# The late expert tiles of a gated transformer block, from 256 rows of one expert to two pieces of 128

## The chip, the cores and the metric

The kernel runs on one NeuronCore of one Trainium2 chip. The core has TensorE (PE in the profile; its weight loads stand apart as PEld), VectorE (DVE), ScalarE (ACT), GpSimd (POOL), SyncE (SP, which here only issues transfers) and 16 DMA engines. The metric is the device time of one execution in microseconds. It is the median of the runs.

## The reference, cut to what matters

x and ctx are 128 sequences of 64 tokens with 128 values each, 8192 tokens in all.

```python
x = x + tanh(g_xattn) * attention(layernorm(x), ctx, ctx)    # 16 heads of 8
z = layernorm(x)                                              # per token
logits = z @ gate_kernel                                      # 8 experts
top_w, top_i = top_k(logits, 2); w = softmax(top_w)
for each token, for each of its two experts n:
    h = silu(z @ w0_kernel[n]) * (z @ w1_kernel[n])           # 128 -> 256
    y += w[n] * (h @ wo_kernel[n])                            # 256 -> 128
x = x + tanh(g_ffn) * y
```

Everything is float32. Each token goes to two of eight experts, so the experts have 16384 rows to work through. How many fall to which expert is known only at run time.

## The kernel before, in words

**Two stages.** The attention stage goes over 64 tiles of 128 tokens in a software pipeline. For each token it also finds the two experts and scatters two copies of the normalised row, with the token's number and weight behind it (130 values, 520 bytes), into `lists` in DRAM: there each expert has a list of its own, filled from the front (POOL, indirect DMA, line 1114). Fills of padding rows (line 294) stand behind each list; their token number is out of bounds, so that their result is dropped.

The expert stage goes over `NET` = 71 tiles of `ET` = 256 rows. A tile belongs to one expert. Since every list but for luck ends within a tile, there are 64 + 7 tiles: 2 x 8192 / 256 and up to seven more. The stages overlap: after 48 token tiles (`EARLY`) a count shows how many full tiles each expert has, and a first table lists `NFULL` = 41 of them, for which all rows are there. A second table, made by DVE while the first expert tiles run (`second_table`, lines 851 to 898), lists the other 30 from the final counts. A table has two rows: the expert of each tile and its first row in `lists`.

**One expert tile t.** Every engine runs the same steps s, each with its own offset:

- SP (`take`, lines 365 to 374) reads the first row from the table into a register, waits until the scatter of tile t - 8 has landed and the outputs of tile t - 6 are made, and issues the load of 256 rows into `zin` (8 buffers).
- PE in step s turns the rows of tile s + 2 (`rows_turned`, L546), multiplies tile s + 1 with the first layer's weights (`first_products`, L556, two matrices of 256 columns into two PSUM banks) and tile s with the second layer's (`second_layer`, L572). For the latter it reads the expert's number into a register (`expert`, recorded at L298) and addresses `wo` with it. A float32 matmul is two passes in the profile, each with its own weight load.
- ACT in step s reads the expert's number of tile s + 2 and copies that expert's two first matrices into `wcur` (L720), does the silu of tile s + 1 (L726) and scales the outputs of tile s by the token's weight (L733).
- DVE in step s copies the turned rows of tile s + 2 (L1015) and multiplies silu and second product of tile s + 1 (`hm`, L1022).
- POOL scatters the 2 x 128 result rows of tile s to `results`, by token number (L1170). In the first 20 steps it also scatters the last eight half tiles of the lists (L1114).

Steps below `steady` = 18 are written out, steps 18 to 49 are a loop of four turns of eight tiles, and the rest is written out again; the order of the work on each engine is the order of these calls.

**The end.** Once all tiles below `NEARLY` = 55 have landed, every result of the first 48 token tiles is in `results`: SP fetches them in 12 chunks of four token tiles (L379), one after each `take`, DVE adds them up in steps from `COMBINE_AT` = 60 on (L1028, L1030), and ACT issues the stores (L739). The last four chunks are fetched when all 71 tiles have landed.

Of the kernel before, what the change touches and what calls it, by code (L numbers as in the profile page):

```python
# [13 lines left out]
P = 128  # L14
# [7 lines left out]
SPARE = E  # L22
# [3 lines left out]
NET = 2 * NT * P // ET + E - 1  # L26
NFULL = 2 * EARLY * P // ET - (E - 1)
NEARLY = 2 * EARLY * P // ET + (E - 1)
# [59 lines left out]
EXPERTS = Pipeline(NET, behind=1, ahead=2, unroll=8, steady=18, turns=4)  # L88
# [34 lines left out]
def flamingo_block(nc, A, out):  # L123
    with ExitStack() as ctx:
# [111 lines left out]
        left = sb("left", [P, E])  # L236
# [10 lines left out]
        tile_no = sb("tile_no", [P, NET])  # L247
# [10 lines left out]
        wcur = sb("wcur", [P, 2, 2, HID])  # L258
# [46 lines left out]
        EARLY_READY, LATE_READY = 11, 20  # L305
# [4 lines left out]
        with nc.Block() as block:  # L310
            @block.sync
            def _(sp):
# [52 lines left out]
                def take(t):  # L365
                    row = sp.value_load(table[0:1, 1, t.val:t.val + 1] if isinstance(t.val, int) else table[0:1, 1, bass.ds(t.val, 1)],
                                        min_val=0, max_val=ZROWS - ET)
# [6 lines left out]
                    sp.dma_start(zin[:, t.buf(8), :, :], lists[bass.ds(row, ET), :].rearrange("(p h) c -> p h c", h=2)).then_inc(z_in[t.buf(8)], 16)  # L374
# [54 lines left out]
            def _(pe):  # L429
# [119 lines left out]
                def first_products(s):  # L549
                    if t := EXPERTS.at(s, 1):  # L550
# [668 lines left out]
```

## Time and profile before

| | us |
|---|---|
| median of 3 runs (lowest, highest) | 565.22 (564.27, 565.32) |
| the profiled execution | 563.8 |
| its span in the profile | 562.0 |
| PE busy | 536.1 |
| ACT busy | 411.7 |
| DVE busy | 401.4 |
| POOL busy | 375.9 |

The span runs from the first to the last instruction of the profiled execution; the 1.8 us around it are in the execution's own time. The busy time of an engine is the time in which at least one of its instructions ran. Register loads, waits and the issuing of transfers are not counted in it. The views used below are the page; the timeline, which gives instructions in order of time with the idle time before them and what ended it; the view of one source line, which also has the sequencer's own instructions (marked q); the waits; and busy times by window.

### The profile page before, as it was taken

The page shows a single profiled execution, that of the slowest core. Times are in us where ns is not written, and L with a number is a line of the kernel's source. Part 1 is how long each engine was busy: PE and PEld are TensorE (multiplying, and loading weights), DVE is VectorE, ACT ScalarE, POOL GpSimd, SP SyncE. Part 2 cuts the span into 40 slices and gives each one's busy share as a digit, 9 for nine tenths or more (in the row PEclk, how much of TensorE's full clock was granted, in tenths as well). Part 3 has the DMA queues.
Part 4 walks back from the last instruction along what each step waited for, and adds up shares of the span by engine and source line. Part 5 has one row for each costly group of instructions (what it writes and reads, how often), then busy time and mean ns, then how long its engine had stood idle before and what let it go on. Part 6 is the DMA issues. An engine that isn't in the chain of part 4 may idle for free.

```text
span 562.0 us, 20142 instructions
## 1 busy us (share of the span) xinstructions
PE 536.1 (95%) x5964; PEld 456.0 (81%) x5965; DVE 401.4 (71%) x1356; ACT 411.7 (73%) x1083; POOL 375.9 (67%) x520
## 2 busy tenths in 40 slices
PE   8999999999999999999999999999899999999960
PEld 6888787888888887888788778998889999999950
DVE  5888988998898998898999875473333333335773
ACT  4788888888888888888999896666566656665630
POOL 3237676767767767677776765777777776667770
PEclk9999999999999999999999999999999999999985
DMA  3652121121222212212212222334333333338997
GB/s 89 207 150 77 55 86 59 52 80 56 66 66 66 75 56 72 69 52 82 60 58 80 78 59 67 100 98 145 112 101 101 106 99 95 94 91 229 314 302 224
DMA packets 70249, 58.00 MB, mean 103 GB/s; under 512 B 8966, under 2 KB 66062, under 8 KB 70192
## 3 DMA queue, kind: packets, MB, share of 16 engines
q1 hardware_dynamic: 52672, 35.98, 22.7%
q0 software_dynamic: 8640, 16.93, 8.9%
q10 hardware_dynamic: 8880, 4.39, 2.6%
q8 instruction: 27, 0.44, 0.4%
q14 instruction: 30, 0.25, 0.1%
HBM read 29.84 MB, written 24.15 MB: 96 GB/s over the span
## 4 chain that ended last, share of the span: by engine, by line
PE 72%; POOL 10%; issue 9%; DMA 4%; DVE 2%; POOLq 1%; ACT 1%; SPq 0%; ACTq 0%; DVEq 0%
PE psO L526 12%; PE psH L466 12%; POOL results L1170 9%; PE psH L556 9%; PE psH L452 7%; PE psH L458 7%; PE psK L504 5%; PE psO L484 3%; PE psX L471 3%; PE psO L498 3%; PE psG L572 2%; PE psO L572 2%; DMA results<-ys,zin 2%; PE psX L508 1%; PE psK L479 1%
## 5 line engine op out<-in xcount | busy, mean ns | idle before, releaser
L1170 POOL DMA_INDIRECT results<-ys,zin x142 | 139.6, 983 | 50.6 <-issue 47.2
L1114 POOL DMA_INDIRECT lists<-zp,dest x128 | 128.1, 1001 | 61.4 <-DVE dest L922 28.9
L556 PE MATMUL psH<-zT,wcur 128*128 128x256 f32 x568 | 134.6, 380 | 0.0
L556 PEld LDWEIGHTS psH<-zT,wcur 128*128 128x128 f32 x568 | 102.4, 190 | 11.2 <-issue 0.2
L1022 DVE TENSOR_TENSOR hm<-psH,hs 128x512 f32<-128x512 f32 x71 | 49.1, 692 | 85.5 <-PE psH L556 52.3
L658 ACT ACTIVATE ex<-psH,rs 128x512 f32<-128x512 f32 x128 | 81.2, 684 | 38.6 <-PE psH L458 38.6
L907 DVE TENSOR_REDUCE mx<-psH 128x8 fp32r<-128x512 f32 x128 | 82.5, 686 | 4.4 <-PE psH L452 0.3
L526 PEld LDWEIGHTS psO<-v,pT 128*64 128x64 f32 x2048 | 65.0, 138 | 25.1 <-issue 23.1
L466 PE MATMUL psH<-ident,ex 128*128 128x128 f32 x512 | 76.4, 282 | 0.1
L526 PE MATMUL psO<-v,pT 128*64 128x64 f32 x2048 | 73.7, 225 | 0.6 <-ACT pT L662 0.6
L1153 POOL TENSOR_TENSOR kvr<-ropA,ropB 128x256 f32<-128x256 f32 x64 | 46.4, 726 | 40.1 <-DVE ropB L984 23.8
L662 ACT COPY pT<-psH 128x512 f32<-128x512 f32 x128 | 72.9, 600 | 0.2
L702 ACT COPY v<-kvr 64x64 f32<-64x64 f32 x256 | 63.3, 247 | 2.3
L466 PEld LDWEIGHTS psH<-ident,ex 128*128 128x128 f32 x512 | 54.0, 140 | 13.2 <-ACT ex L658 10.2
L458 PE MATMUL psH<-mx,minus 128*128 128x256 f32 x256 | 59.8, 320 | 0.0
L720 ACT COPY wcur<-w 128x512 f32 x71 | 43.8, 617 | 11.5 <-issue 7.9
L733 ACT ACTIVATE ys<-psO,zin 128x128 f32<-128x128 f32 x72 | 22.5, 363 | 32.9 <-PE psO L572 32.9
L932 DVE TENSOR_TENSOR kmask<-psK,hmask 128x512 f32<-128x512 f32 x64 | 44.0, 687 | 3.1 <-PE psK L479 2.5
L733 ACT ACTIVATE ys<-psG,zin 128x128 f32<-128x128 f32 x70 | 21.9, 363 | 32.9 <-PE psG L572 31.9
L452 PE MATMUL psH<-kmask,qT 32*64 32x256 f32 x1024 | 44.6, 400 | 0.0
L726 ACT ACTIVATE hs<-psH 128x512 f32<-128x512 f32 x71 | 42.0, 591 | 2.8 <-PE psH L556 2.8
L458 PEld LDWEIGHTS psH<-mx,minus 128*128 128x128 f32 x256 | 38.5, 190 | 3.6 <-DVE mx L907 0.2
(157 smaller groups left out, 991.8 us busy)
## 6 DMA issues: line engine op xcount, KB each, us to landing
zin<-lists SPq DMA_DIRECT2D x71, 130.0 KB, 2.1
yy<-results SPq DMA_DIRECT2D x16, 512.0 KB, 5.8
xres<-x1r SPq DMA_DIRECT2D x32, 128.0 KB, 2.2
out_dram<-xres ACTq DMA_DIRECT2D x16, 256.0 KB, 3.9
xring<-in_x_dram SPq DMA_DIRECT2D x31, 128.0 KB, 2.2
cring<-in_ctx_dram SPq DMA_DIRECT2D x31, 128.0 KB, 2.3
results<-ys,zin POOLq DMA_INDIRECT x142, 2.5
lists<-pad SPq DMA_DIRECT2D x16, 130.0 KB, 3.4
```

Source lines behind the costliest of these rows:

```text
L452: last = pe.matmul(psH[h][c, g % 2, 0:256], qT[r, t.buf(2), c], kmask[r, t.buf(2), :, c], start=True, stop=False, skip_group_check=True)
L458: last = pe.matmul(psH[h][:, g % 2, 0:256], minus[:, :], mx[:, 4 * g:4 * g + 4].unsqueeze(2).broadcast_to([P, 4, S]), start=False, stop=Tr ...
L466: last = pe.transpose(psH[h][:, n // 2, o:o + P], ex[:, t.buf(2), h, n * P:(n + 1) * P], ident[:, :])
L526: last = pe.matmul(psO[b * S:(b + 1) * S, n * VW:n * VW + VPAD], pT[:, t.buf(2), n // 4, o:o + S], v9[:, t.buf(4), b, n * VW:n * VW + VPAD ...
L556: last = pe.matmul(bank[t.buf(2)][:, k * ET:(k + 1) * ET], wcur[:, t.buf(2), a, k * P:(k + 1) * P], zT[:, t.buf(2), :], start=True, stop=True)
L658: nc.scalar.activation(ex[:, t.buf(2), h, :].rearrange("p (g c) -> p g c", g=2), psH[h][:, :, 0:256], ACT.Exp, scale=rs[:, t.buf(4) // 2, ...
L662: nc.scalar.copy(pT[:, t.buf(2), h, :].rearrange("p (g c) -> p g c", g=2), psH[h][:, :, 256:512]).then_inc(p_sb[h], 1)
L702: last = nc.scalar.copy(dst, src)
L907: nc.vector.tensor_reduce(mx[:, 8 * h:8 * h + 8].rearrange("p (g n) -> p g n", g=2), psH[h][:, :, 0:256].rearrange("p g (n k) -> p g n k", ...
L1022: nc.vector.tensor_tensor(hm[:, t.buf(2), :, :].rearrange("p k t -> p (k t)"), psB[t.buf(2)][:, :], hs[:, t.buf(2), :], ALU.mult).then_inc ...
L1114: nc.gpsimd.indirect_dma_start(lists, bass.IndirectOffsetOnAxis(ap=dest[:, t.buf(4), j:j + 1], axis=0), zp[:, t.buf(4), j, :], None).then_ ...
L1170: nc.gpsimd.indirect_dma_start(results, bass.IndirectOffsetOnAxis(ap=zin[:, t.buf(8), h, D:D + 1].bitcast(U32), axis=0), ys[:, t.buf(8), h ...
```

## The change

Tiles 0 to 40 stay. From tile 41 on (the 42nd) a tile of 256 rows is two pieces of 128 rows, each with an expert and a first row of its own in the table. Lists are thus rounded up to 128 rows behind the first table's tiles, and 68 tiles hold them: (128 + 7 + 1) // 2. The second table has 54 entries, one for each piece, in place of 30. A late tile is loaded with two transfers; ACT copies two experts' matrices; the first layer's matmuls are made for 128 columns at a time, each with the weights of its piece; the second layer uses each piece's expert. `NEARLY` goes from 55 to 52. The loop has two turns instead of four, so that no late tile lies in it. PE and ACT wait for the second table at the steps 41 and 39 instead of 17 and 15.

```diff
-SPARE = E
+SPARE = E // 2
 ZROWS = E * CAP + SPARE * ET
 ROW = D + 2
 EARLY = 3 * NT // 4
-NET = 2 * NT * P // ET + E - 1
 NFULL = 2 * EARLY * P // ET - (E - 1)
-NEARLY = 2 * EARLY * P // ET + (E - 1)
+NET = (2 * NT + E - 1 + 1) // 2
+NEARLY = (2 * EARLY + E - 1 + 1) // 2
+PIECES = 2 * (NET - NFULL)
+NTAB = NFULL + PIECES
...
-EXPERTS = Pipeline(NET, behind=1, ahead=2, unroll=8, steady=18, turns=4)
+EXPERTS = Pipeline(NET, behind=1, ahead=2, unroll=8, steady=18, turns=2)
...
-        past = sb("past", [P, NET - NFULL, SEG])
-        hop = sb("hop", [P, 2, NET - NFULL, SEG])
-        tfl = sb("tfl", [P, 2, NET])
-        first_row = sb("first_row", [P, NET])
-        table = sb("table", [P, 2, NET], U32)
+        past = sb("past", [P, PIECES, SEG])
+        hop = sb("hop", [P, 2, PIECES, SEG])
...
-        wcur = sb("wcur", [P, 2, 2, HID])
+        wcur = sb("wcur", [P, 2, 2, 2, HID])
...
-        def expert(eng, t):
-
-            return eng.value_load(table[0:1, 0, t.val:t.val + 1] if isinstance(t.val, int) else table[0:1, 0, bass.ds(t.val, 1)],
-                                  min_val=0, max_val=E - 1)
+        def late(t):
+
+            return t.turn is None and t.k >= NFULL
+
+        def entry(t, h):
+            if late(t):
+                k = NFULL + 2 * (t.k - NFULL) + h
+                return slice(k, k + 1)
+            return slice(t.val, t.val + 1) if isinstance(t.val, int) else bass.ds(t.val, 1)
+
+        def rows_there(eng, t):
+
+            if late(t):
+                slot = range(t.buf(8), t.k + 1, 8)
+                eng.wait_ge(z_in[t.buf(8)], sum(32 if n >= NFULL else 16 for n in slot))
+            else:
+                wait_slot(eng, z_in, t, 16)
+
+        def expert(eng, t, h=0):
+
+            return eng.value_load(table[0:1, 0, entry(t, h)], min_val=0, max_val=E - 1)
...
-                    row = sp.value_load(table[0:1, 1, t.val:t.val + 1] if isinstance(t.val, int) else table[0:1, 1, bass.ds(t.val, 1)],
-                                        min_val=0, max_val=ZROWS - ET)
+                    rows = [sp.value_load(table[0:1, 1, entry(t, h)], min_val=0, max_val=ZROWS - (P if late(t) else ET))
+                            for h in range(2 if late(t) else 1)]
                     wait_slot(sp, y_out, t, 32, back=8)
                     carry(sp)
                     if t.turn is not None or t.k >= 8:
                         wait_for(sp, y_sb, t, back=6)
                     carry(sp)
                     carry(sp)
-                    sp.dma_start(zin[:, t.buf(8), :, :], lists[bass.ds(row, ET), :].rearrange("(p h) c -> p h c", h=2)).then_inc(z_in[t.buf(8)], 16)
+                    if late(t):
+                        for h in range(2):
+                            sp.dma_start(zin[:, t.buf(8), h, :], lists[bass.ds(rows[h], P), :]).then_inc(z_in[t.buf(8)], 16)
+                    else:
+                        sp.dma_start(zin[:, t.buf(8), :, :], lists[bass.ds(rows[0], ET), :].rearrange("(p h) c -> p h c", h=2)).then_inc(z_in[t.buf(8)], 16)
...
-                        wait_slot(pe, z_in, t, 16)
+                        rows_there(pe, t)
...
-                                last = pe.matmul(bank[t.buf(2)][:, k * ET:(k + 1) * ET],
-                                                 wcur[:, t.buf(2), a, k * P:(k + 1) * P],
-                                                 zT[:, t.buf(2), :], start=True, stop=True)
+                                for h, c in enumerate((slice(0, P), slice(P, ET)) if late(t) else (slice(0, ET),)):
+                                    last = pe.matmul(bank[t.buf(2)][:, k * ET + c.start:k * ET + c.stop],
+                                                     wcur[:, t.buf(2), h, a, k * P:(k + 1) * P],
+                                                     zT[:, t.buf(2), c], start=True, stop=True)
...
-                        e = expert(pe, t)
+                        e = [expert(pe, t, h) for h in range(2)] if late(t) else [expert(pe, t)] * 2
...
-                                                 wo[:, bass.ds(e, 1), k, :].squeeze(1), start=(k == 0), stop=(k == 1))
+                                                 wo[:, bass.ds(e[h], 1), k, :].squeeze(1), start=(k == 0), stop=(k == 1))
...
-                    if static(s, EXPERTS.steady - 1):
+                    if static(s, NFULL):
...
-                        e = expert(act, t)
+                        e = [expert(act, t, h) for h in range(2 if late(t) else 1)]
                         wait_for(act, b_ps, t, back=2)
-                        nc.scalar.copy(wcur[:, t.buf(2), :, :], w01[:, bass.ds(e, 1), :, :].squeeze(1)).then_inc(w_done, 1)
+                        for h, n in enumerate(e):
+                            last = nc.scalar.copy(wcur[:, t.buf(2), h, :, :], w01[:, bass.ds(n, 1), :, :].squeeze(1))
+                        last.then_inc(w_done, 1)
...
+                        nc.vector.tensor_copy(ecnt[:, :], psG[:, 0:E])
...
-                        nc.vector.tensor_scalar(ntu[:, 1, :], ntu[:, 0, :], ET.bit_length() - 1, None, ALU.logical_shift_right).then_inc(late_table, 1)
                         dve.wait_ge(late_table, 4)
+                        nc.vector.tensor_scalar(ntu[:, 1, :], ntu[:, 0, :], P.bit_length() - 1, None, ALU.logical_shift_right).then_inc(late_table, 1)
+                        nc.vector.tensor_scalar(ecu[:, 1, :], ecu[:, 0, :], P.bit_length() - 1, None, ALU.logical_shift_right).then_inc(late_table, 1)
+                        dve.wait_ge(late_table, 6)
                         nc.vector.tensor_copy(ntf[:, :], ntu[:, 1, :]).then_inc(late_table, 1)
-                        dve.wait_ge(late_table, 5)
-                        nc.vector.tensor_tensor(left[:, :], ntf[:, :], seg_len[:, 0:E], ALU.subtract).then_inc(late_table, 1)
+                        nc.vector.tensor_copy(ecf[:, :], ecu[:, 1, :]).then_inc(late_table, 1)
+                        nc.vector.tensor_scalar(seg_len[:, 0:E], seg_len[:, 0:E], 2.0, None, ALU.mult).then_inc(late_table, 1)
                     if n == 2:
-                        dve.wait_ge(late_table, 6)
-                        nc.vector.tensor_scalar(seg_len[:, E:2 * E], left[:, :], 1.0, None, ALU.min).then_inc(late_table, 1)
-                        dve.wait_ge(late_table, 7)
-                        nc.vector.tensor_tensor(seg_len[:, 2 * E:SEG], left[:, :], seg_len[:, E:2 * E], ALU.subtract).then_inc(late_table, 1)
-                        nc.vector.scalar_tensor_tensor(out=seg_row[:, E:2 * E], in0=seg_len[:, 0:E], scalar=float(ET), in1=seg_row[:, 0:E],
+                        dve.wait_ge(late_table, 9)
+                        nc.vector.tensor_tensor(seg_len[:, E:2 * E], ecf[:, :], seg_len[:, 0:E], ALU.subtract).then_inc(late_table, 1)
+                        nc.vector.tensor_tensor(seg_len[:, 2 * E:SEG], ntf[:, :], ecf[:, :], ALU.subtract).then_inc(late_table, 1)
...
-                        nc.vector.tensor_tensor(past[:, :, :], seg_end[:, :].unsqueeze(1).broadcast_to([P, late, SEG]),
-                                                tile_no[:, NFULL:NET].unsqueeze(2).broadcast_to([P, late, SEG]), ALU.is_le).then_inc(late_table, 1)
+                        dve.wait_ge(late_table, 16)
+                        nc.vector.tensor_tensor(past[:, :, :], seg_end[:, :].unsqueeze(1).broadcast_to([P, PIECES, SEG]),
+                                                tile_no[:, NFULL:NTAB].unsqueeze(2).broadcast_to([P, PIECES, SEG]), ALU.is_le).then_inc(late_table, 1)
```

The remaining edits name the new buffers, make the two iotas of the tables in two parts each, and renumber the semaphore counts of `second_table` (`LATE_READY` 23 instead of 20).

## Rows read from the trace of the kernel before

**Rows 1.** The profile page: busy time of PE, and the clock granted in 40 slices

```profile
PE 536.1 (95%) x5964; PEld 456.0 (81%) x5965; DVE 401.4 (71%) x1356; ACT 411.7 (73%) x1083; POOL 375.9 (67%) x520
...
PEclk9999999999999999999999999999999999999985
```

**Rows 2.** Timeline of one late tile, all engines: start, duration in us, [idle before]

```profile
492.30 1.05 PE L572 MATMUL psO<-wo,hm 128*128 x8
492.50 0.69 DVE L1022 TENSOR_TENSOR hm<-psH,hs 128x512 f32<-128x512 f32 x1 [1.30 <-PE psH L556]
...
493.19 0.38 PE L546 MATMUL psK<-ident,zin 128*128 128x128 f32 x2
...
493.39 0.62 ACT L733 ACTIVATE ys<-psO,zin 128x128 f32<-128x128 f32 x2 [1.01 <-PE psO L572]
493.40 1.89 PE L556 MATMUL psH<-zT,wcur 128*128 128x256 f32 x8
...
494.10 0.62 ACT L720 COPY wcur<-w 128x512 f32 x1
...
494.62 0.59 ACT L726 ACTIVATE hs<-psH 128x512 f32<-128x512 f32 x1
494.83 0.97 POOL L1170 DMA_INDIRECT results<-ys,zin  x1 [0.59 <-issue]
...
495.13 1.05 PE L572 MATMUL psG<-wo,hm 128*128 x8
```

**Rows 3.** Timeline of PE alone from 403 to 420 us

```profile
404.37 0.44 PE L546 MATMUL psX<-ident,zin 128*128 128x128 f32 x2 [1.45 <-DMA zin<-lists]
...
416.26 0.44 PE L546 MATMUL psX<-ident,zin 128*128 128x128 f32 x2 [0.32 <-DMA zin<-lists]
...
418.50 1.05 PE L572 MATMUL psO<-wo,hm 128*128 x8
```

**Rows 4.** Timeline of POOL from 360 to 366 us

```profile
361.10 0.97 POOL L1170 DMA_INDIRECT results<-ys,zin  x1 [0.30 <-issue]
362.38 0.97 POOL L1170 DMA_INDIRECT results<-ys,zin  x1 [0.30 <-issue]
363.66 0.96 POOL L1114 DMA_INDIRECT lists<-zp,dest  x1 [0.30 <-issue]
```

**Rows 5.** Line 298 on PE's sequencer, 492.2 to 493.1: min/median/max ns, first and last start

```profile
L298 PEldq TENSOR_LOAD <-table x1: 297/297/297, 492.3 to 492.3; - x1
...
L298 PEldq SEQ_ASSERT  x1: 18/18/18, 492.9 to 492.9; - x1
```

**Rows 6.** Line 572 on PE's sequencer, 492 to 495 us

```profile
L572 PEldq FUSED_REGOPS  x2: 46/46/46, 493.2 to 493.4; - x2
```

**Rows 7.** Register loads of line 298 on PE, 430 to 520, then 520 to 542

```profile
L298 PEldq TENSOR_LOAD <-table x32: 297/302/419, 430.4 to 517.9; - x32
...
L298 PEldq TENSOR_LOAD <-table x8: 302/618/1217, 520.7 to 539.3; - x8
```

**Rows 8.** Timeline of ACT near the end: a store's issue

```profile
535.97 0.39 ACTq L739 DMA_DIRECT2D out_dram<-xres  x1
```

**Rows 9.** Timeline of DVE from 370 to 378 us

```profile
377.02 0.89 DVE L894 TENSOR_REDUCE tfl<-hop 128x30 f32<-128x720 f32 x1
```

**Rows 10.** Waits of SP, 430 to 500: us in total, times, longest us

```profile
SPq L120 <- DMA results<-ys,zin: 22.3, 26, 2.0
```

**Rows 11.** Timeline of SP from 506 to 532 us

```profile
508.83 0.44 SPq L379 DMA_DIRECT2D yy<-results  x1
...
530.38 1.77 SPq L379 DMA_DIRECT2D yy<-results  x2
```

**Rows 12.** Busy time of each engine in a window, then granted clock, DMA share, GB/s

```profile
core 0: us, PE busy (x) PEld busy (x) DVE busy (x) ACT busy (x) POOL busy (x), PEclk, DMA share, GB/s
530.00:540.00 10.00, 10.00 (x64) 9.23 (x63) 8.40 (x15) 6.18 (x15) 6.79 (x7) 1.00 1.04 334
```

**Rows 13.** Waits of SP from 500 us to the end

```profile
SPq L120 <- DMA results<-ys,zin: 11.6, 8, 2.2
```

More of the change, by code:

```diff
@@ L235, in flamingo_block @@
         ntf = sb("ntf", [P, E])
-        left = sb("left", [P, E])
+        ecnt = sb("ecnt", [P, E])
+        ecu = sb("ecu", [P, 2, E], U32)
+        ecf = sb("ecf", [P, E])
         seg_len = sb("seg_len", [P, SEG])
@@ L246, in flamingo_block @@
         padrow = sb("padrow", [P, E], U32)
-        tile_no = sb("tile_no", [P, NET])
+        tile_no = sb("tile_no", [P, NTAB])
         early_past = sb("early_past", [P, NFULL, E])
         early_hop = sb("early_hop", [P, NFULL, E])
-        past = sb("past", [P, NET - NFULL, SEG])
-        hop = sb("hop", [P, 2, NET - NFULL, SEG])
-        tfl = sb("tfl", [P, 2, NET])
-        first_row = sb("first_row", [P, NET])
-        table = sb("table", [P, 2, NET], U32)
+        past = sb("past", [P, PIECES, SEG])
+        hop = sb("hop", [P, 2, PIECES, SEG])
+        tfl = sb("tfl", [P, 2, NTAB])
+        first_row = sb("first_row", [P, NTAB])
+        table = sb("table", [P, 2, NTAB], U32)
         warm = sb("warm", [P, 1])
@@ L849, in second_table @@
                 def second_table(n):
-                    late = NET - NFULL
                     if n == 0:
@@ L888, in second_table @@
+                        nc.vector.tensor_tensor(hop[:, 0, :, :], past[:, :, :], expert_step[:, :].unsqueeze(1).broadcast_to([P, PIECES, SEG]),
                                                 ALU.mult).then_inc(late_table, 1)
[L889 removed]
+                        nc.vector.tensor_tensor(hop[:, 1, :, :], past[:, :, :], jump[:, :].unsqueeze(1).broadcast_to([P, PIECES, SEG]),
                                                 ALU.mult).then_inc(late_table, 1)
@@ L891, in second_table @@
                     if n == 6:
-                        dve.wait_ge(late_table, 16)
-                        nc.vector.tensor_reduce(tfl[:, 0, NFULL:NET], hop[:, 0, :, :], AX_X, ALU.add).then_inc(late_table, 1)
-                        nc.vector.tensor_reduce(tfl[:, 1, NFULL:NET], hop[:, 1, :, :], AX_X, ALU.add).then_inc(late_table, 1)
+                        dve.wait_ge(late_table, 19)
+                        nc.vector.tensor_reduce(tfl[:, 0, NFULL:NTAB], hop[:, 0, :, :], AX_X, ALU.add).then_inc(late_table, 1)
@@ L895, in second_table @@
+                        nc.vector.tensor_reduce(tfl[:, 1, NFULL:NTAB], hop[:, 1, :, :], AX_X, ALU.add).then_inc(late_table, 1)
                     if n == 7:
-                        dve.wait_ge(late_table, 18)
-                        nc.vector.tensor_scalar(table[:, 0, NFULL:NET], tfl[:, 0, NFULL:NET], float(E - 1), None, ALU.min).then_inc(late_table, 1)
-                        nc.vector.tensor_tensor(table[:, 1, NFULL:NET], tfl[:, 1, NFULL:NET], first_row[:, NFULL:NET], ALU.add).then_inc(late_table, 1)
+                        dve.wait_ge(late_table, 21)
@@ L900, in rows @@
+                        nc.vector.tensor_scalar(table[:, 0, NFULL:NTAB], tfl[:, 0, NFULL:NTAB], float(E - 1), None, ALU.min).then_inc(late_table, 1)
+                        nc.vector.tensor_tensor(table[:, 1, NFULL:NTAB], tfl[:, 1, NFULL:NTAB], first_row[:, NFULL:NTAB], ALU.add).then_inc(late_table, 1)
                 def rows(t):
@@ L1088, in _ @@
                 pool.wait_ge(pad_ready, 1)
-                nc.gpsimd.iota(tile_no[:, :], pattern=[[1, NET]], base=0, channel_multiplier=0,
+                nc.gpsimd.iota(tile_no[:, 0:NFULL], pattern=[[1, NFULL]], base=0, channel_multiplier=0,
+                               allow_small_or_imprecise_dtypes=True)
+                nc.gpsimd.iota(tile_no[:, NFULL:NTAB], pattern=[[1, PIECES]], base=2 * NFULL, channel_multiplier=0,
                                allow_small_or_imprecise_dtypes=True).then_inc(e_const, 1)
-                nc.gpsimd.iota(first_row[:, :], pattern=[[ET, NET]], base=0, channel_multiplier=0,
+                nc.gpsimd.iota(first_row[:, 0:NFULL], pattern=[[ET, NFULL]], base=0, channel_multiplier=0,
+                               allow_small_or_imprecise_dtypes=True)
+                nc.gpsimd.iota(first_row[:, NFULL:NTAB], pattern=[[P, PIECES]], base=2 * NFULL * P, channel_multiplier=0,
                                allow_small_or_imprecise_dtypes=True).then_inc(e_const, 1)
```

24 lines of the change are left out of this document (11 added, 13 removed).

## The prediction, made before the changed kernel was run

> **What bounds the kernel now.** The page comes first: TensorE (PE) is busy 95% of the span, and the granted clock stands at nine tenths or more of 2.4 GHz up to the last two of 40 slices [rows 1]. So PE looks like the bound, but a busy share is an average, and the change touches only the last stage. The timeline of one expert tile there comes next [rows 2]: second layer (L572), two transposes (L546), eight matmul passes of the first layer (L556), next second layer, without a gap. From the second layer at 418.50 [rows 3] to that at 492.30 [rows 2] there are 26 tiles in 73.80 us, 2.84 us each. In each, PE spends 1.73 us on L556 (493.40 to 495.13, 8 x 0.216), 0.89 on L572 (492.30 to 493.19, 8 x 0.111) and 0.21 on L546. ScalarE (ACT) is free for 1 us before each result, GpSimd (POOL) for 0.59.
>
> Is PE the bound of the whole stage? No: at 404.37 and 416.26 it waited 1.45 and 0.32 us for rows [rows 3]. The reader should see POOL behind this: its scatters follow each other every 1.28 us, and eight scatters of the last lists (L1114) are mixed in [rows 4]. Two scatters of results are 2.56 us a tile, so POOL gains back 0.28 us a tile once the extra ones are done, and by the tile of rows 2 it idles. Up to about the 26th tile POOL sets the pace, afterwards PE. The change replaces tiles from the 42nd on: all of them lie in PE's part.
>
> **What is removed.** NET goes from 71 to 68: three tiles of 2.84 us, and NEARLY and COMBINE_AT move down by three too (55 to 52, 60 to 57), so that the fetches and sums keep their place relative to the last tile, and what lies behind it stays. Gain: 3 x 2.84 = 8.5 us.
>
> **PE's added work.** In 27 late tiles the first layer is split by columns: 16 passes of 128 columns, each with its weights, in place of 8 of 256. No first-layer pass of 128 columns is in the trace, but L572 is the same shape (128x128 weights, 128 columns, float32) at 0.111: 16 x 0.111 = 1.78 against 1.73, +0.05 a tile. The bounds are 16 x 0.107 (L546's, no more than before) and 16 x 0.112: 0 to +0.06. I take 0.05: 27 x 0.05 = 1.4 us. Late period: 2.89.
>
> **PE's second register load.** A late tile reads two expert numbers. The first costs PE's sequencer 0.30 us for the load at 492.3 and, with the range check at 492.9, about 0.67 in all, 0.37 beside the load [rows 5]. Then come the address computations of L572, at 493.2 and 493.4 [rows 6]. This load belongs to the second layer that runs at 495.13. It starts when PE begins the second layer before, with 8 + 2 + 8 = 18 matmuls still queued: so the sequencer runs some 16 to 18 matmuls ahead, no more. Today these are 2.83 us of work over about 1.1 us of sequencer time. After the change the 16 short L556 passes fill that room alone: the loads can start only when the second transpose's weights are taken, 0.9 us after L572's start; they take 2 x (0.37 + load), and some 0.25 follows until the first matmul is handed over. With today's lead of weights (0.1) the loop of the sequencer is 0.9 + 0.74 + 2 x load + 0.35 = about 2.0 + 2 x load. At 0.30 that is 2.6, hidden under 2.89 with 0.3 to spare. But from 520 us on the same load takes 0.62 in the median of eight, up to 1.22 [rows 7]: 2.0 + 1.24 = 3.25, or 0.36 over 2.89. Bounds for the seven or eight tiles there: 0 (only the first of the pair is slow and the next catches up) to 8 x 0.36 = 2.9; I take the middle, 1.4.
>
> The Trainium skill, DMA: Bandwidth & Descriptors, Latency and other measured facts, gives a register load a floor of about 600 ns. The trace disagrees for most of the stage, 0.30, and comes to such a figure only at the end. By that rule the loop would be 3.2 in all 27 tiles and the gain gone (rival 2). The skill's Advanced Engine Details and Errata, Engine Queue Depths, gives TensorE a queue of 64; counted as weight loads and matmuls, the trace shows about half. By that depth the second load would be hidden even at 1.2 us (rival 1).
>
> **ACT.** It copies weights twice. One copy occupies it 0.52 (494.10 to the silu at 494.62). The second load adds about 0.6 (493.39 to 494.10 is 0.71 today, load and checks). So silu starts 0.71 + 0.6 + 1.04 = 2.35 after the outputs and leaves ACT at about 2.85: just under 2.89. Silu comes 1.1 us later than today; the product (hm, 0.69) behind it would end about 3.7 after the outputs' start, and its second layer starts at 4.7 (today hm ends 2.6 after, its consumer starts 4.6 after). Hidden, with 1 us left. In the last 11 steps ACT also issues the stores, 0.39 each [rows 8], ahead of its loads. It can work through that, since a late ACT finds its result waiting and loads while the silu still runs: 0. If that cover is gone: 0.4 x 11 = 4.3 us.
>
> **VectorE (DVE).** The second table gets 54 x 24 = 1296 elements for 720. At 0.90 us each [rows 9] the five operations grow by about 0.6 each, 3 us together, in three steps of 2.84, two of them ahead of a tile's transposed input. One tile is late by up to 1.3 us around 378 us. That lies in POOL's part: PE then waits less for rows at 404.37 [rows 3]. 0 us; 1.3 if POOL were not the pace there. The small added operations (one copy in the attention stage, some on eight elements) I put at 0.1 together, the two extra iotas and four fewer fills at 0.
>
> **SP and DMA.** A late tile is two transfers of 128 x 520 B for one of 128 x 1040 B: the same bytes, one more issue of 0.33 and a second load, about 1.1 us more of SP a tile. From 430 to 500 SP spends 22.3 us in 26 waits for scatters to land [rows 10], most of them behind the load, and it works up to eight tiles ahead: hidden. In the last steps it also fetches results; the fetches come every 3.1 us (seven steps from 508.83 to 530.38) [rows 11], slower than PE's tiles, with the DMA engines full [rows 12]. In its eight waits for scatters there SP spends 11.6 us, 1.4 each [rows 13], which would hold the 1.1; but the second issue comes behind the wait. Bounds 0 and 8 x 0.5 = 4 us; as the waits are the longer I take 0.3.
>
> **Sum.** -8.5 + 1.4 + 1.4 + 0.3 + 0.1 = -5.3 us. Against the profiled execution, 563.8 (span 562.0), that is 558.5; against the median of the runs shown, 565.22, it is **559.9 us**. I give the second.
>
> **Rivals.** (1) *Only the matmuls cost.* The slow loads and SP stay hidden: -8.5 + 1.4 + 0.1 = -7.0, 558.2. For it: the 0.3 us to spare in PE's loop, and SP's waits. Against it: loads of 0.62. The Trainium skill's queue of 64 would lead here too.
> (2) *PE waits for its register loads, or ACT for its own, in every late tile.* Place: PE's sequencer between first and second layer, tiles 41 to 67. Price: with loads of 0.62 throughout, 3.25 - 2.84 = 0.41 x 27 = 11.1, against 8.5: +2.6, 567.9, slower. It decides from a period of 2.84 + 8.5/27 = 3.16, that is from loads of 0.58. Against it: 32 loads of 0.30 in the median from 430 to 520 [rows 7]. It is what the Trainium skill's floor of a register load (the page named above) would do here.
> (3) *The same, partly*: period 3.0 to 3.1, because handing over costs more than I count or ACT's 2.85 is really 3.0. 27 x 0.2 = 5.4 instead of 1.4: -8.5 + 5.4 + 1.8 = about -1.5, 563.7. From -2 up to no change.
> (4) *The end is DMA's.* With the engines full from 510 on, three tiles less do not bring the fetches forward; then the end stays at its place, and only slack goes: about 565. Against it: the first fetch waits for the scatters of the first NEARLY tiles, which come three tiles earlier, and the last four fetches start only behind the last scatter, in the old kernel as in the new.
>
> **Chances.** Forecast (-4 to -6.5): 0.45. Rival 1 (-6.5 to -8): 0.25. Loss between (-1.1 to -4, rival 3): 0.13. Rival 4 or rival 3 at its end, within 1.1 us: 0.08. Rival 2: 0.09. A measurement of this kernel tells about 0.2%, 1.1 us, from no change: faster 0.83, same 0.08, slower 0.09. Range: low, near rival 1 without a price for the matmuls (556.8), 557.0; high, rival 3, 563.7; outside are rival 2, rival 4 and a little below: 2 in 10.
>
> **What would show it.** L572 to L572 of late tiles 2.89 before the fetches and 2.9 to 3.3 after; 16 passes of L556 in 1.78; two loads behind each other on PE with the first at the second transpose; ACT's wait for PE shrunk from 1.0 to nearly 0; silu 2.35 behind the outputs; SP's waits shorter. Wrong would be: a gap of PE before L572 in tiles 41 to 58, loads of 0.6 there, or the last scatter not earlier by 5 us.

## The result, and the profile after

Twenty runs of each kernel were compared: 561.86 us after (559.71 to 564.4), 565.18 before (563.4 to 567.21). The ratio is 0.9946, 95% interval 0.9936 to 0.9957. By it the change takes 3.05 us off (2.4 to 3.6), where 5.3 were predicted; the medians are 3.3 apart. The profiled execution took 560.92 us, its span is 558.8.

The page, busy times and granted clock (after; it answers to [rows 1]):

```profile
PE 531.9 (95%) x6126; PEld 456.5 (82%) x6127; DVE 399.4 (71%) x1354; ACT 419.4 (75%) x1098; POOL 370.3 (66%) x516
...
PEclk9999999999999999999999999999999999999995
```

PE is busy 4.2 us less, ACT 7.7 us more. The timeline of PE in the first late tiles (after; start, duration in us):

```profile
459.77 1.06 PE L598 MATMUL psO<-wo,hm 128*128 x8
460.66 0.38 PE L571 MATMUL psK<-ident,zin 128*128 128x128 f32 x2
460.88 1.95 PE L582 MATMUL psH<-zT,wcur 128*128 128x128 f32 x16
462.67 1.06 PE L598 MATMUL psG<-wo,hm 128*128 x8
```

L571, L582 and L598 are the old L546, L556 and L572. From second layer to second layer is 2.90 us. The sixteen first-layer passes take 462.67 - 460.88 = 1.79, against 1.73 for the eight of [rows 2]. This goes on without a gap for nineteen tiles. In the last eight it does not (PE's timeline, after):

```profile
515.95 2.02 PE L582 MATMUL psH<-zT,wcur 128*128 128x128 f32 x16
518.13 1.15 PE L598 MATMUL psO<-wo,hm 128*128 x8 [0.17 <-issue]
...
519.55 2.05 PE L582 MATMUL psH<-zT,wcur 128*128 128x128 f32 x16
521.55 1.15 PE L598 MATMUL psG<-wo,hm 128*128 x8
...
532.28 2.05 PE L582 MATMUL psH<-zT,wcur 128*128 128x128 f32 x16 [0.33 <-ACT wcur L747]
534.53 1.15 PE L598 MATMUL psG<-wo,hm 128*128 x8 [0.20 <-issue]
...
537.31 1.06 PE L598 MATMUL psO<-wo,hm 128*128 x8
539.25 1.15 PE L598 MATMUL psG<-wo,hm 128*128 x8 [0.89 <-ACT ys L761]
```

Follow one late pair. The second layer at 518.13 should have come at 517.74, 2.90 behind that at 514.84; it is 0.39 late. What held it is not in PE's own timeline but in its sequencer. The instructions there, from the trace (start, us, ns, engine):

```
515.987   383 Tensor  TENSOR_LOAD  L320 <-table
516.720   763 Tensor  TENSOR_LOAD  L320 <-table
516.361   302 Scalar  TENSOR_LOAD  L320 <-table
516.920  1074 Scalar  TENSOR_LOAD  L320 <-table
517.297   961 Sync    TENSOR_LOAD  L387 <-table
...
519.622   303 Tensor  TENSOR_LOAD  L320 <-table
```

PE's second register load ends at 517.48, and behind it come its checks and the addresses of L598. ACT's second load ends at 517.99, its weight copies start at 518.36, and the next L582 waits for them (timeline of all engines, after):

```profile
518.12 0.97 PEld L598 LDWEIGHTS psO<-wo,hm 128*128 128x128 f32 x8 [0.35 <-issue]
...
518.36 1.14 ACT L747 COPY wcur<-w 128x512 f32 x2 [1.49 <-PE psH L582]
...
519.54 0.19 PEld L582 LDWEIGHTS psH<-zT,wcur 128*128 128x128 f32 x1 [0.28 <-ACT wcur L747]
```

So in this pair each engine's second load has a part. L598 is 0.39 late behind PE's own loads, the first of which had itself begun 0.24 late. Then L582 follows 1.42 behind L598 in place of 1.11, 0.31 late by `wcur`. PE's next loads (519.62, the second of 0.72) begin only behind that L582, and the next L598 loses another 0.21: 0.39 and 0.52 over 2.90 in two tiles. The waits of the last stretch (after, 511 to 541; us in total, times, longest) show the same two causes. `issue` before a weight load is PE's sequencer that hands over late, here behind its register loads:

```profile
PEld psG L598 <- issue: 1.5, 2, 1.1
PEld psH L582 <- ACT wcur L747: 1.1, 3, 0.6
PE psG L598 <- ACT ys L761: 0.9, 1, 0.9
PEld psO L598 <- issue: 0.4, 1, 0.4
```

The 1.1 of `issue` and the 0.9 of `ys` are one gap, that ahead of the last tile. It is PE's own, since the outputs that this tile needs, those of the tile two before, were ready at 536.35: no L582 covers the last tile's two loads (0.80 and 0.30, from 537.26 on). The sequencer of PE over the two stretches (line 320, which [rows 7] has as line 298; min/median/max ns, first and last start):

```profile
L320 PEldq TENSOR_LOAD <-table x42: 295/300/482, 439.9 to 510.0; - x42
...
L320 PEldq TENSOR_LOAD <-table x16: 297/304/947, 516.0 to 538.4; - x16
```

The median stays at 0.30 to the end: of sixteen loads, five are slow (0.51 to 0.95), four of them the second of their pair. The windows (after; the one of 530 to 540 answers to [rows 12]) show when this begins, with the DMA engines full:

```profile
core 0: us, PE busy (x) PEld busy (x) DVE busy (x) ACT busy (x) POOL busy (x), PEclk, DMA share, GB/s
440.00:500.00 60.00, 60.00 (x496) 58.77 (x495) 22.05 (x42) 43.25 (x99) 42.62 (x45) 1.00 0.35 98
...
510.00:520.00 10.00, 9.79 (x85) 9.33 (x84) 6.98 (x12) 6.78 (x17) 6.75 (x7) 1.00 0.97 283
520.00:530.00 10.00, 9.99 (x87) 9.62 (x86) 7.73 (x14) 6.95 (x17) 5.83 (x6) 1.00 1.03 316
530.00:540.00 10.00, 8.58 (x72) 7.97 (x71) 8.18 (x14) 5.63 (x13) 6.15 (x6) 1.00 0.98 304
```

PE is busy for sixty of sixty us, and from 530 on for 8.58 of ten. SP's waits from 430 to 500, where [rows 10] had 22.3 us in one row, and the last scatter of POOL:

```profile
SPq L122 <- DMA results<-ys,zin: 9.5, 8, 1.4
SPq L122 <- ACT ys L761: 7.2, 13, 0.8
```

```profile
543.90 0.97 POOL L1203 DMA_INDIRECT results<-ys,zin  x1 [0.30 <-issue]
```

Before, that scatter was issued at 547.10: it is 3.2 us earlier. From its end to the end of the span both kernels need 13.9 us.

**The account of the two profiled executions**, by the first second-layer matmul of each tile:

| | before | after | difference |
|---|---|---|---|
| first tile starts | 341.19 | 342.31 | +1.12 |
| first to 41st tile | 117.05 | 117.46 | +0.41 |
| 41st to the ninth last | 62.44 (22 x 2.84) | 55.07 (19 x 2.90) | -7.37 |
| ninth last to last | 20.68 | 24.42 | +3.74 |
| last tile to last scatter | 5.74 | 4.64 | -1.10 |
| from there to the end | 14.9 | 14.9 | 0 |

They sum to -3.2, the difference of the spans. Each column is one execution.

### The profile page after: what moved, and what is told of

The parts are those of the page before. It is cut to its first block, busy times and chain, and to the rows that moved or that the text cites. A ratio compares the mean times of both kernels' runs of the same rounds, so it can differ in the third digit from the quotient of the medians.

```text
span 558.8 us, 20707 instructions
## 1 busy us (share of the span) xinstructions
PE 531.9 (95%) x6126; PEld 456.5 (82%) x6127; DVE 399.4 (71%) x1354; ACT 419.4 (75%) x1098; POOL 370.3 (66%) x516
## 4 chain that ended last, share of the span: by engine, by line
PE 86%; ACT 3%; issue 3%; DMA 3%; ACTq 2%; DVE 2%; POOL 1%; POOLq 0%; SPq 0%; DVEq 0%
PE psH L582 17%; PE psO L551 12%; PE psH L491 12%; PE psH L477 7%; PE psH L483 7%; PE psK L529 5%; PE psG L598 4%; PE psO L598 4%; PE psO L509 3%; PE psX L496 3%; PE psO L523 3%; ACTq L320 1%; PE psX L533 1%; PE psK L504 1%; PE psX L534 1%
## 5 line engine op out<-in xcount | busy, mean ns | idle before, releaser
L1203 POOL DMA_INDIRECT results<-ys,zin x136 | 133.8, 984 | 52.2 <-issue 42.1
L582 PE MATMUL psH<-zT,wcur 128*128 128x128 f32 (+1 forms) x760 | 131.0, 321 | 1.1 <-issue 0.7
L582 PEld LDWEIGHTS psH<-zT,wcur 128*128 128x128 f32 x760 | 109.5, 191 | 8.9 <-issue 1.1
L1051 DVE TENSOR_TENSOR hm<-psH,hs 128x512 f32<-128x512 f32 x68 | 47.0, 691 | 91.7 <-PE psH L582 46.6
L747 ACT COPY wcur<-w 128x512 f32 x95 | 56.0, 616 | 23.9 <-issue 19.3
L754 ACT ACTIVATE hs<-psH 128x512 f32<-128x512 f32 x68 | 40.2, 591 | 3.4 <-PE psH L582 3.3
L529 PE MATMUL psK<-wT,xcT 128*128 128x256 f32 x128 | 38.7, 384 | 1.1 <-DVE kmask L961 1.1
L678 ACT ACTIVATE zp<-x1r,nmr,rs 128x256 f32<-128x256 f32 x64 | 38.5, 602 | 1.5
```

Of the source, the lines that this page charges most:

```text
L529: pe.matmul(psK[:, 0:2 * D], xcT[:, t.buf(8), P:2 * P], wT[:, 1:3, :], start=True, stop=True).then_inc(kv_ps, 1)
L582: last = pe.matmul(bank[t.buf(2)][:, k * ET + c.start:k * ET + c.stop], wcur[:, t.buf(2), h, a, k * P:(k + 1) * P], zT[:, t.buf(2), c], st ...
L1203: nc.gpsimd.indirect_dma_start(results, bass.IndirectOffsetOnAxis(ap=zin[:, t.buf(8), h, D:D + 1].bitcast(U32), axis=0), ys[:, t.buf(8), h ...
```

## The experiments

Twelve runs were made of six kernels, in four groups, each on one chip. The kernel before took 664.6, 684.4, 564.9 and 663.1 us there: three groups met chips on which it takes 1.17 to 1.21 times as long, and there PE doesn't set the pace of the tiles. So the third group, on a chip like the one of the result, carries the verdicts; its four kernels are those of the first. The changed kernel itself was not in it: it is compared with the others by its ratio of 0.9946 from the first comparison. Each ratio is to the kernel before on the same chip, with its 95% interval.

### Three tiles fewer and nothing else

```diff
-NET = 2 * NT * P // ET + E - 1
+NET = 2 * NT * P // ET + E - 1 - 3
-NEARLY = 2 * EARLY * P // ET + (E - 1)
+NEARLY = 2 * EARLY * P // ET + (E - 1) - 3
```

> The kernel before with 68 tiles in place of 71 and nothing else changed (the last three tiles' rows are left out of the computation). Theory (the three tiles are worth 2.84 us each, and what follows the last tile stays where it was relative to it): 8.5 us less than before, a ratio of 0.985. Rival 4 (the transfers set the end): 0 to 2 us less.

Measured: 654.46 us against 664.56, ratio 0.9832 [0.9807, 0.9856].

> The kernel before with 68 tiles in place of 71 and nothing else; three tiles' work (and so three tiles' rows) is left out. Where TensorE sets the pace, three tiles at a period of 2.84 us make 8.5 us less: 556.7 against 565.2 (ratio 0.985). If the end belonged to the transfers, it would be within 2 us of the kernel before.

Measured: 556.67 us, ratio 0.985 [0.9824, 0.9876], that is -8.5 us (the span is 8.2 less). The first term of the sum holds. Rival 4, by which the end is the transfers', falls: the last scatter is issued at 537.91, 9.2 earlier, and 1.0 of that is lost again behind it.

### The split matmuls alone

```diff
-EXPERTS = Pipeline(NET, behind=1, ahead=2, unroll=8, steady=18, turns=4)
+EXPERTS = Pipeline(NET, behind=1, ahead=2, unroll=8, steady=18, turns=2)
...
+                                late = t.turn is None and t.k >= NFULL
+                                for c in (slice(0, P), slice(P, ET)) if late else (slice(0, ET),):
-                                last = pe.matmul(bank[t.buf(2)][:, k * ET:(k + 1) * ET],
+                                    last = pe.matmul(bank[t.buf(2)][:, k * ET + c.start:k * ET + c.stop],
                                                  wcur[:, t.buf(2), a, k * P:(k + 1) * P],
-                                                 zT[:, t.buf(2), :], start=True, stop=True)
+                                                     zT[:, t.buf(2), c], start=True, stop=True)
```

The late steps are written out (turns=2), and the tables are those of the kernel before; the first sentence of the second text below says otherwise, and is wrong in that.

> The kernel before with its 71 tiles of one expert; only the first layer's matmuls from tile 41 on are made for 128 columns at a time, and the loop has two turns, so that these tiles are written out. Theory: 0.06 us for each of 30 late tiles, 1.7 us more than before, period 2.90, no gaps of TensorE. Rival (handing over twice as many matmuls costs something at the end, where register loads are slow): 3 to 5 us more.

Measured: 667.69 us against 664.56, ratio 1.0041 [1.0024, 1.0058].

> The kernel before, its 71 tiles kept, from the 42nd on with the products of a tile made in pieces of 128 columns and the tables built as in the changed kernel, but with one expert number for a tile, so without any further load of a number. If the split matmuls are all that the late tiles cost, the rise is 30 tiles x 0.06 = 1.8 us (567.0, ratio 1.003), and the rest of the late tiles' price, which the trace of the changed kernel puts at 3.7 us in the last eight, comes from the second loads. If the split alone brings that too, +4 to +5 us (569.5).

Measured: 566.3 us, ratio 1.0023 [1.0004, 1.0041], +1.3 us. Every interval between second layers from the 41st tile on is 2.90, the last eight included, up to the last two of 2.68 and 1.03. The last eight sum to 21.1 us against 20.7 before. PE's timeline at the end (split alone):

```profile
536.76 1.06 PE L574 MATMUL psG<-wo,hm 128*128 x8
539.66 1.06 PE L574 MATMUL psO<-wo,hm 128*128 x8
542.34 1.06 PE L574 MATMUL psG<-wo,hm 128*128 x8
```

So the split costs what its 0.06 a tile says, and the gaps of the last eight tiles are not its doing.

### One expert number for both pieces

```diff
-                        e = [expert(pe, t, h) for h in range(2)] if late(t) else [expert(pe, t)] * 2
+                        e = [expert(pe, t)] * 2
...
-                        e = [expert(act, t, h) for h in range(2 if late(t) else 1)]
+                        e = [expert(act, t)] * (2 if late(t) else 1)
```

> The changed kernel, in which TensorE and ScalarE read one expert number for a late tile and use it for both pieces (the second piece is computed with the first one's expert). Theory (the 3.7 us lost in the last eight tiles come from the second register load on the two sequencers): about 3 us less than the changed kernel, a ratio to before of 0.989 to 0.990, last eight tiles at 2.9. Rival (ScalarE's second copy, the second transfer and the full DMA engines do it): no more than 1 us less than the changed kernel, 0.994.

Measured: 661.8 us against 664.56, ratio 0.9955 [0.9923, 0.9987].

> As the run of the same kernel above (one expert number for both pieces on TensorE and ScalarE), now beside the changed kernel: by the theory 3 us less than the changed kernel (0.5%), by the rival less than 1 us.

Measured: 682.49 us against 684.42, ratio 0.9899 [0.9851, 0.9947].

> The changed kernel with one expert number read for both pieces of a tile by TensorE and ScalarE, so that the second piece is multiplied with the first piece's weights. If the second loads cost the 3.7 us that the last eight tiles took more than before, less 0.5 for the split, this gains 2 to 3.2 us on the changed kernel (559.2, ratio to the kernel before 0.989 to 0.990). If the loads cost nothing and the end is the split's or the transfers', it is the changed kernel again (0.9946).

Measured: 559.87 us, ratio 0.9904 [0.9878, 0.993], so 2.4 us less than the changed kernel (0.9946 [0.9936, 0.9957]; the two intervals just don't overlap, and the 2.4 could be 0.8 to 4). PE's timeline at the end (one number):

```profile
529.19 1.06 PE L598 MATMUL psO<-wo,hm 128*128 x8
...
532.09 1.06 PE L598 MATMUL psG<-wo,hm 128*128 x8
...
534.77 1.06 PE L598 MATMUL psO<-wo,hm 128*128 x8
535.98 1.15 PE L598 MATMUL psG<-wo,hm 128*128 x8 [0.15 <-DVE hm L1051]
```

The 2.90 stand to the end. The last eight intervals sum to 21.28 us, against 24.42 in the changed kernel: 3.14 us are the second reads' of PE and ACT together (load, check and addresses). The span shrinks by 2.1 only, since POOL is then the later at the end: its last scatter stands 5.94 behind the last tile and not 4.64. SP's second load, both transfers of a tile and ACT's second copy are still in this kernel, so they cost PE nothing here. The windows of the two kernels have nearly the same DMA share (1.04 and 1.03 from 520 to 530), so it isn't that the DMA engines are less full (one number):

```profile
520.00:530.00 10.00, 10.00 (x92) 10.00 (x91) 7.91 (x14) 8.11 (x18) 7.96 (x7) 1.00 1.04 316
```

### The loads moved apart

The whole of the changed kernel; on PE the first number is read ahead of the first products, on ACT the second is read behind the first copy.

```diff
-                def second_layer(s):
+                def second_layer(s, e0=None):
-                        e = [expert(pe, t, h) for h in range(2)] if late(t) else [expert(pe, t)] * 2
+                        e = [e0, expert(pe, t, 1)] if late(t) else [expert(pe, t)] * 2
...
+                    t0 = EXPERTS.at(s, 0)
+                    e0 = expert(pe, t0, 0) if t0 and late(t0) else None
...
-                        e = [expert(act, t, h) for h in range(2 if late(t) else 1)]
-                        wait_for(act, b_ps, t, back=2)
-                        for h, n in enumerate(e):
+                        for h in range(2 if late(t) else 1):
+                            n = expert(act, t, h)
+                            if h == 0:
+                                wait_for(act, b_ps, t, back=2)
```

> The changed kernel, complete; TensorE reads the first number ahead of the first layer's matmuls and the second behind them, ScalarE reads the second number behind the first copy. Theory: each load on TensorE then has 1.8 us of queued matmuls over it, ScalarE's second load lies under the 0.52 us copy: most of what one number for both pieces gives, 2 to 3 us less than the changed kernel, ratio 0.989 to 0.991. Rival (slow loads are not the cause): 0.994.

Measured: 665.28 us against 664.56, ratio 0.9997 [0.997, 1.0024].

> As the run of the same kernel above (the register loads apart, nothing left out), now beside the changed kernel: by the theory 2 to 3 us less than the changed kernel, by the rival less than 1 us.

Measured: 682.05 us against 684.42, ratio 0.9951 [0.9912, 0.999].

> The whole of the changed kernel, with the second number's load moved: on TensorE the first number is read ahead of the tile's first products and the second behind them, on ScalarE the second is read behind the first copy. If what costs is that two loads stand one behind the other while the queue behind them runs empty, this gains 1 to 3 us on the changed kernel (ratio 0.989 to 0.993). If each load costs its own time wherever it stands, it is the changed kernel again (0.9946).

Measured: 560.52 us, ratio 0.9921 [0.9893, 0.9948], 1.4 us less than the changed kernel, with overlapping intervals; the trace has 22.59 us in the last eight intervals, 1.8 less. PE's timeline at the end (loads moved):

```profile
529.55 1.06 PE L598 MATMUL psO<-wo,hm 128*128 x8
530.44 0.38 PE L571 MATMUL psK<-ident,zin 128*128 128x128 f32 x2
531.01 2.02 PE L582 MATMUL psH<-zT,wcur 128*128 128x128 f32 x16 [0.18 <-issue]
```

The gap now stands ahead of L582, where the first load went. Ten of PE's 25 loads from 500 us on took over 0.4, more than the five of 26 in the changed kernel, and yet less time was lost. That the order counts, and not only the number of slow loads, is what this one pair of traces says; the times don't prove it. Of the kernels measured that compute every row whatever the lists' lengths, this has the lowest time.

### The changed kernel again, beside two of these

> The changed kernel once more, as it is, beside the next two on one chip. Theory and rivals alike: a ratio to before of 0.9946 if the chip runs the kernels as in the first comparison; on a chip where the kernel before takes 664 us, something else than the counted work sets the pace of every second tile, and the ratio may be nearer to 1.

Measured: 684.19 us against 684.42, ratio 0.9991 [0.995, 1.0032]. On this chip the order is the same as on that of the third group, one number (0.9899), moved (0.9951), changed (0.9991), but the changed kernel's own gain is gone.

### One number on TensorE alone

```diff
-                        e = [expert(pe, t, h) for h in range(2)] if late(t) else [expert(pe, t)] * 2
+                        e = [expert(pe, t)] * 2
```

> The changed kernel, with TensorE alone reading one expert number for both pieces of a late tile (the second piece's last product takes the first piece's weights); ScalarE reads both, as in the changed kernel. Reading one number on both engines gave 0.9904 of the kernel before, the changed kernel is at 0.9946. If it is TensorE's own second load that costs, this is 0.990 to 0.9915, and the late tiles keep 2.90 us to the end. If it is ScalarE's, whose weights come too late, it is 0.9935 to 0.995, with intervals over 3 us in the last eight tiles. If each has its part, between the two.

Measured: 662.93 us against 663.12, ratio 0.9983 [0.9955, 1.0012]. Inconclusive: on this chip a pair of late tiles takes 7.2 us, not 5.8, as it did in the first group with one number on both engines, so PE does not set the pace there. How the loss divides between PE's load and ACT's no run shows; the trace of the changed kernel shows only that both have a part.

## Why the prediction was right in direction and short in size

The range (557.0 to 563.7) holds the result, and the direction is right. But the gain of 3.05 lies outside the forecast's own band (4 to 6.5, chance 0.45), in the one from 1.1 to 4, which had 0.13. Term by term:

- **Three tiles, -8.5.** Right. Alone they are worth 8.5 us (0.985).
- **The split, +1.4.** Right. The late period is 2.90 where 2.89 was predicted, and alone the split costs 1.3 us [0.2 to 2.3] (all 71 tiles kept, so in thirty tiles).
- **PE's second register load: a mis-sized term.** The place was right. The first of the pair starts at 460.68, 0.91 behind L598's start, as predicted. The 0.3 us to spare are about right too: in the pair followed above the two loads began 0.24 later and took 0.55 longer together than in an undisturbed tile, and L598 came only 0.39 late, so 0.4 was to spare. The prediction took 1.4 us for this and 0.3 for SP, 1.7 together. The last eight intervals took 3.74 more than before, of which 0.4 is the split; without the second loads 3.14 of it are gone in the trace, and 2.4 us in the times. The failed step is the one that costed the term from PE alone, as eight times 0.36, halved. The duration that it took, 0.62 for every load at the end, was too high: the median remained 0.30, and five of sixteen on PE were slow. What it left out is that PE also stands behind ACT's second loads. A late `wcur` holds L582, and it holds PE's loads too: in five of the last eight tiles, PE's first load began 0.12 to 0.15 behind the end of the copy (519.49 and 519.62 above).

  The queue was a condition of this term. At the start of the load at 460.68 PE had 33 matmuls and weight loads ahead of it, and in the kernel before, at 492.3, as many. The Trainium skill, Advanced Engine Details and Errata, Engine Queue Depths, allows TensorE 64 entries. The traces don't show so many, if each matmul and each weight load is an entry. Nor could a deeper queue have let the load start a tile earlier, as rival 1 needs: it stands behind L582's wait for `wcur`, which was ready at 460.35, so some 0.2 us were to be had (an estimate from the 0.12 to 0.15 above).
- **ACT, 0.** Right in the undisturbed tiles: its copies start 1.12 behind the outputs (1.31 predicted; timeline of a tile below), and PE never waits. But most of the cover was gone. From 498 to 513 `wcur` was ready 0.30 to 0.46 us before L582 took it, against 1.3 to 1.5 in the kernel before. In the last eight the 0 is wrong. First came the stores, whose cover the prediction trusted. ACT issues one ahead of its loads, and the copies then start 1.69 behind the outputs, with both loads still at 0.28 and 0.29 (ACT's timeline, after):

```profile
513.03 0.37 ACT L761 ACTIVATE ys<-psO,zin 128x128 f32<-128x128 f32 x1
513.04 0.46 ACTq L767 DMA_DIRECT2D out_dram<-xres  x1
513.30 0.36 ACT L761 ACTIVATE ys<-psO,zin 128x128 f32<-128x128 f32 x1
514.72 1.14 ACT L747 COPY wcur<-w 128x512 f32 x2 [1.06 <-issue]
```

  This ended the cover: that copy is the one that held PE's load at 515.99. Then ACT's second loads took 0.49 to 1.07 in six tiles, and PE waited 1.1 us for `wcur`. The prediction let PE's loads be slow there and kept ACT's at 0.6 with their checks. With one number the stores stand there too, and `wcur` keeps 0.24 to 0.58 us of cover. The undisturbed tile:

```profile
492.38 0.59 ACT L754 ACTIVATE hs<-psH 128x512 f32<-128x512 f32 x1
...
492.86 0.62 ACT L761 ACTIVATE ys<-psG,zin 128x128 f32<-128x128 f32 x2
...
493.98 1.14 ACT L747 COPY wcur<-w 128x512 f32 x2 [0.50 <-issue]
```

- **DVE's table, 0 (1.3 at most).** The operations grew as predicted, 1.50 us against the 0.89 of [rows 9], and held back two tiles by 0.3 and 0.9 us (DVE's timeline, after, then PE's):

```profile
378.25 1.50 DVE L922 TENSOR_REDUCE tfl<-hop 128x54 f32<-128x1296 f32 x1
379.66 1.50 DVE L923 TENSOR_REDUCE tfl<-hop 128x54 f32<-128x1296 f32 x1
381.07 0.42 DVE L1044 COPY zT<-psK 128x256 f32<-128x256 f32 x1
```

```profile
381.59 1.97 PE L582 MATMUL psH<-zT,wcur 128*128 128x256 f32 x8 [0.68 <-issue]
```

  Later waits for rows took back some 0.8 of that in this execution (2.5 us of them against 3.3 before). From the first tile to the 41st the kernels with the old table took 117.05, 116.57 and 117.23 us, those with the new one 117.46, 117.85 and 117.66: 0.7 more in the mean. By the times, what the changed kernel has besides tiles, split and second loads costs 0.9904 - 0.985 - 0.0023 = 0.0031, 1.8 us, with an uncertainty (2.3) larger than itself. Of this 0.7 is placed; the rest is open.
- **SP, 0.3.** Its waits for scatters shrank from 22.3 to 9.5 us, those for `ys` from 16.9 to 7.2, and it held up nothing in the undisturbed tiles. With its second load and issue still there, one number has its 2.90 to the end, so this term is nearer to 0.
- **Not in the sum: POOL behind the last tile.** The last scatters follow each other every 1.28 us. Before, the last tiles ended 2.62 and 1.04 us apart, faster than POOL scatters; now they come 2.78 and 1.95 apart, and POOL catches up 1.1 us. This is why 1.1 of the 3.7 us that PE lost in the last eight intervals did not reach the last scatter.
- **Not in the sum: the start.** The profiled execution after began its first tile 1.1 us later. Most of this, 0.9, is no part of the change (last section).

The terms by times: -8.5 + 1.3 + 1.8 + 2.4 = -3.0. This closes by construction, since 1.8 is what the others leave over. The last two were put at 0.1 and 1.7, so by the times 0.7 of the missing 2.3 us is the second loads' and 1.7 is the remainder, most of which no run places. By the two traces it is +1.4 for the second loads (3.1 for 1.7), +0.2 for the split, +0.4 up to the 41st tile, +1.1 at the start and -1.1 behind the last tile, 2.0 together. That the total comes out as near as it does is in part luck: of the terms that the sum left out, those at the start and behind the last tile cancel in the traced execution.

Of the rivals, (1) falls, since second loads cost; (2) falls, since the period is 2.90 and not 3.16. (3), something between, is nearest to the size, but its mechanism, a longer period in all late tiles, is not what happened (its sum, -8.5 + 5.4 + 1.8, is -1.3 and not the -1.5 that gave the range its upper end). (4) falls. The Trainium skill, DMA: Bandwidth & Descriptors, Latency and other measured facts, gives a register load about 600 ns as its least; 42 loads on PE had a median of 0.300 here, so rival 2, which hung on it, had no ground on this stage.

## What to carry to other kernels

Where a bound engine reads a register from memory for each tile, find how many instructions it has queued when the read begins, and add a second read only where that queue covers both at the durations seen when the DMA engines are full. Do the same for every engine that reads and that the bound one waits for: how long before its use is the result ready, and is that more than a slow read takes? Look at the last tiles by themselves: a change that is worth its price in twenty tiles of a steady stretch can lose as much in the eight in which the stores and fetches run. If two reads are needed, it is worth trying to put work between them (1.4 us less here, which the noise does not rule out as nothing).

## What the runs showed of the hardware that was not expected

**Slow register loads come in some executions and not in others.** In the changed kernel, from 516 us on, PE's first loads took 0.30 to 0.38 but for the last tile's 0.80, its second ones 0.76, 0.72, 0.31, 0.51, 0.30, 0.95, 0.30 and 0.30; ACT's first ones 0.28 to 0.35, its second ones 1.07, 0.68, 0.56, 0.49, 0.83 and 0.78. So there the second was mostly the slow one. But single loads can be as slow. With one load a tile and the DMA engines as full, six of PE's last eight took 0.46 to 1.22 in the kernel before and five of eight 0.51 to 0.74 with three tiles fewer, but one of eight (0.85) with one number and none of nine (0.38 at most) with the split alone. In the kernel before the slow loads cost PE nothing: it is busy throughout [rows 12]. What makes a load slow is not shown; the slow ones of PE, ACT and SP fall together (516.7, 516.9 and 517.3).

**When TensorE reaches its pace at the start varies.** In PE's timeline of the kernel before, six filler matmuls at 4.66 took 1.04 us; after:

```profile
4.85 1.49 PE L470 MATMUL psO<-ident 128*128 128x128 f32 x6
```

They start 0.213 us apart at first and 0.109 later. The trace's record of the granted clock begins, at 1.00 (2.4 GHz), at 6.84 us after and at 5.10 before; what was granted ahead of it is not recorded, but the matmuls go at half the pace there (the windows view gives 1.00 for it all the same). The six took 0.82, 1.04, 1.15, 1.49 and 1.49 in five traces of kernels with the old tables and 0.82 to 1.49 in nine with the new, so it is not the change's. At half the pace the 1.74 us between the two records cost 0.87 (an estimate), most of the 1.12 by which the first expert tile was later. In the six traces from chips of this kind that tile comes later the later the record begins: 341.08, 341.19, 341.27, 341.78, 341.89 and 342.31 for 4.73, 5.10, 5.28, 5.77, 6.28 and 6.84, though the last three are the kernels with the new tables. It is a reason to compare from a common event and not from the start.

**Chips differ.** On the chips where the kernel before took 664 us, PE's matmuls are as fast, but the other engines start late on what it has made. Timeline of all engines (split alone, first group):

```profile
564.91 1.06 PE L574 MATMUL psO<-wo,hm 128*128 x8
...
565.80 0.38 PE L546 MATMUL psK<-ident,zin 128*128 128x128 f32 x2
...
568.90 0.63 ACT L735 ACTIVATE ys<-psO,zin 128x128 f32<-128x128 f32 x2 [3.91 <-PE psG L574]
568.94 0.42 DVE L1017 COPY zT<-psK 128x256 f32<-128x256 f32 x1 [2.24 <-remote]
```

The matmuls of `psO` end at 565.97 and the transposes at 566.18; ACT and DVE start on them at 568.90 and 568.94, 2.8 to 2.9 us later, where on the other chip `ys` starts 0.15 behind L598 (492.71 and 492.86). The semaphore for which DVE waits there has no increment in the trace between the end of these transposes and 568.92, so the signal is late and not DVE. Why, the traces don't say. There the changed kernel gained nothing (0.9991), though three tiles fewer by themselves gained 1.7% on another such chip.
